# Two attention-and-FFN layers: DMA transposes for the second FFN's levels, its down product behind the next queries, and a new order at both ends of the first FFN

## The chip, the cores and the metric

One NeuronCore of a Trainium2 chip runs the whole kernel. The metric is the device time of one execution in microseconds; below it is the median of three runs.

## The reference

The input is `x` (8 x 256 x 512) with a context of the same shape. Two layers follow each other. Only what the change touches is shown.

```python
# layer 0: causal attention over context and self keys (16 heads of 128, 4 kv heads), then
h = bitlinear(x, w1)                    # w1 2048 x 512, ternary weights, 8-bit activations
x = x + bitlinear(square(relu(h)), w2)  # w2 512 x 2048
# layer 1: single-head attention over the 256 context rows, only the 54 largest scores kept
scores = coef * (x @ Wq.T) @ ctx.T ; thr = top_k(scores, 54)[-1]
x = x + softmax(where(scores < thr, -inf, scores)) @ ctx @ Wo.T
# layer 1: gated FFN with quantized activations
g = silu(bit_linear(x, w_gate)) * bit_linear(x, w_up)          # 2048 wide
x = x + bit_linear(rms_norm(g, ln_weight), w_down)
# in each quantized product: levels = round(x * 127 / max|x|), weights = clip(round(w / mean|w|), -1, 1)
```

## The kernel before

The 2048 rows are 16 tiles n of 128 rows, or 8 pairs (the attention of both layers works on pairs). Each engine runs a program that is written out by hand, in order, and the engines meet only in semaphores; no engine can pass a wait of its own. All DMAs are issued from one queue, SyncE's (SP), which is just as strictly in order. There are three stages.

1. **First attention**, from 0 to about 878 us. It is not changed.
2. **First FFN** (`ffn0`), to about 1189 us. For each tile: `pe_y` multiplies the attention's output by `wo` in four parts (L1349), `dve_norm` adds and normalizes (L1517 is the first step, L1534 the last, which rounds to levels `xh`), `pe_x_turn` transposes them (L1366), `act_xq` copies them out of PSUM (L1463), `pe_up` is the first product (L1378), VectorE takes the maxima (L1562), `act_relu` and `act_square` follow on ScalarE, `dve_hh` rounds, a DMA transposes (`sp_h_turn`, L1288, two of 128 x 1024 a tile), `pe_down` is the second product (L1389) and `dve_x2` adds it to the row. Into this the second layer's three weight matrices are woven: 48 visits k, in each of which SP loads a chunk of 512 KB (`sp_w`, L1269) into one of three slots and ScalarE passes over it (`act_l`, L1438 for the sums of absolute values, L2666 and L2668 for the levels). The slots held chunks 4 to 6 of the first layer's own second weight until ScalarE had made levels of them.
3. **Second layer** (`layer1`), to the end. Its loop runs over s. In a round s the queries and scores of pair s, the rest of the attention of pair o = s - 1, and the gated FFN of the tiles n = 2(s - 2) and n + 1 are interleaved. Per round TensorE does, in this order: gate and up products of tile n (L1925, four quarters j; the first half of the next queries, `pe_xb(s, 0)`, L1828, before j = 2), the way down of tile n - 1 (L1952), the transpose of the masked weights (`pe_xd`, L1859, which waits for `dve_pm`, L2276), the second half of the queries (`pe_xb(s, 1)`), the weighted sum (`pe_xe`, L1875), transposes, scores (L1844), the output product (`pe_xf`, L1890), gate and up of tile n + 1, and the way down of tile n. A quarter j may start only when VectorE's `dve_h` (L2309) of quarter j - 2 has freed its PSUM banks. On VectorE the six rounds that find the 54th largest score (L2265, L2268) are spread over the two gate-and-up passes: rounds 0 to 2 of pair s over that of tile n + 1, rounds 3 to 5 over the next tile's, and `dve_pm` comes after them. Rounds with everything in them are s = 3 to 7.

The FFN's levels `hh` (fp16) are made in two halves, by `pool_levels` (L2507) and `act_levels` (L2110). `pe_h_turn` transposes each half with eight matmuls into PSUM (L1945, between the quarters of the next tile's gate and up), and `act_hT` (L2116) copies it from there to `hT`, which `pe_down` reads.

## Time and profile before

| | |
|---|---|
| median of three runs | 1566.73 us (1563.74 to 1568.1) |
| profiled execution | 1566.82 us, its span 1565.5 us |
| TensorE busy | 1491.3 us, 95% |
| VectorE, ScalarE, GpSimd busy | 73%, 61%, 44% |
| mean granted TensorE clock | 0.986 of 2.4 GHz |

Times on the profile's axis run from the first instruction to the last; the profiled execution took 1.3 us more than that span. Busy time overlaps, since matmuls are pipelined: the rate of an engine is read from the starts of its instructions, not from their lengths.

### The profile page before, as it was taken

The numbers are of one execution on the slowest core, as the hardware profiler recorded it, in microseconds if no ns is written. First come the engines' busy times: TensorE is split into PE (matmuls) and PEld (weight loads), VectorE is DVE, ScalarE is ACT, GpSimd is POOL, SyncE is SP. The second block draws the span as 40 slices with busy tenths as digits, with TensorE's granted clock in tenths as the row PEclk, the third lists the DMA queues.
The fourth block names the chain that finished last, engine by engine and source line by source line (L and its number), as shares of the span: only waits on it lengthen the run. The fifth ranks groups of instructions, "written<-read, shape, count | busy, mean of one in ns | idle before, by whom it ended". The sixth has DMA issues, their size and how long they took to land. (4 is left out here: it accounts for less than half of the span.)

```text
span 1565.5 us, 26196 instructions
## 1 busy us (share of the span) xinstructions
PE 1491.3 (95%) x8637; PEld 1166.0 (74%) x8637; DVE 1136.6 (73%) x2966; ACT 960.5 (61%) x2470; POOL 693.6 (44%) x832
## 2 busy tenths in 40 slices
PE   7999999999999999999999969999998799999988
PEld 6778888888888888888887636666666566666653
DVE  6787787777776877777787735565566988888774
ACT  5666666666666666666667725555555676666655
POOL 4565555555555555556576200000005455555444
PEclk9999999999999999999999988999998999999999
DMA  7011111111111111111336767888785301111000
GB/s 277 27 42 55 41 68 41 41 68 48 48 59 45 60 42 41 68 45 51 122 125 265 266 184 232 273 273 253 254 233 171 110 21 55 55 48 41 28 14 28
DMA packets 84327, 165.09 MB, mean 105 GB/s; under 512 B 39392, under 2 KB 39520, under 8 KB 82784
## 3 DMA queue, kind: packets, MB, share of 16 engines
q1 hardware_dynamic: 84192, 163.41, 30.6%
q8 instruction: 70, 1.15, 0.3%
q14 instruction: 65, 0.53, 0.1%
HBM read 113.05 MB, written 41.94 MB: 99 GB/s over the span
## 5 line engine op out<-in xcount | busy, mean ns | idle before, releaser
L617 ACT ACTIVATE Pt<-Pt,small 128x384 f32<-128x384 f32 (+1 forms) x256 | 173.1, 684 | 106.0 <-DVE small L877 105.9
L368 PE MATMUL bank<-wq,xT 128*128 128x512 f32 x768 | 208.2, 406 | 0.8 <-DVE wq L772 0.8
L421 PE MATMUL bank<-PT,vv 128*128 128x512 f32 x672 | 199.4, 405 | 5.0 <-DVE PT L862 4.1
L1135 POOL TENSOR_SCALAR Pt<-Pt,small 128x384 f32<-128x384 f32 (+1 forms) x256 | 164.8, 657 | 78.9 <-DVE small L885 78.9
L877 DVE CUSTOM_DVE_ANT_0 Pt<-quad,mask,small 128x384 f32<-128x384 f32 (+1 forms) x256 | 171.7, 680 | 30.5 <-PE quad L398 29.1
L1349 PE MATMUL bank<-wq,ot 128*128 128x512 f32 x768 | 181.8, 394 | 1.4 <-DVE xr L1517 1.4
L862 DVE TENSOR_TENSOR PT<-quad,PT 128x512 fp32r<-128x512 f32 x224 | 153.8, 687 | 38.4 <-ACT PT L609 38.0
L1349 PEld LDWEIGHTS bank<-wq,ot 128*128 128x128 f32 x768 | 143.8, 188 | 33.3 <-issue 1.5
L368 PEld LDWEIGHTS bank<-wq,xT 128*128 128x128 f32 x768 | 137.8, 190 | 26.3 <-DVE wq L772 1.9
L1123 POOL TENSOR_TENSOR t<-t 128x512 f32<-128x512 f32 x64 | 83.7, 1308 | 144.2 <-DVE t L843 144.2
L1635 POOL TENSOR_TENSOR cl<-cl,fixed 128x1 f32<-128x1 f32 x16 | 8.8, 552 | 296.4 <-DVE cl L1523 296.4
L421 PEld LDWEIGHTS bank<-PT,vv 128*128 128x128 f32 x672 | 116.4, 189 | 29.3 <-DVE PT L862 10.5
L609 ACT CAST PT<-quad 128x512 fp32r<-128x512 f32 x224 | 128.9, 591 | 7.5 <-PE quad L408 7.5
L408 PE MATMUL quad<-fixed,Pt 128*128 128x128 f32 x896 | 129.4, 273 | 0.6 <-POOL Pt L1135 0.6
L408 PEld LDWEIGHTS quad<-fixed,Pt 128*128 128x128 f32 x896 | 109.6, 140 | 24.3 <-POOL Pt L1135 2.0
L625 ACT CAST OT<-bank 128x512 fp32r<-128x512 f32 x64 | 37.6, 588 | 137.9 <-PE bank L421 137.9
L2521 POOL TENSOR_TENSOR bhw<-bh,lnw 128x512 f32<-128x512 f32 x64 | 81.9, 1279 | 81.8 <-DVE bh L2309 81.7
L396 PE MATMUL quad<-kT,qT 128*128 128x384 f32 (+1 forms) x256 | 99.3, 388 | 2.2 <-DVE small L877 0.8
L1129 POOL TENSOR_TENSOR small<-small,fixed 128x4 f32<-128x4 f32 x64 | 66.2, 1034 | 72.3 <-DVE small L849 72.2
L338 PE MATMUL bank<-wkc,cT 128*128 128x256 f32 x744 | 97.0, 287 | 0.6 <-issue 0.6
L338 PEld LDWEIGHTS bank<-wkc,cT 128*128 128x128 f32 x744 | 90.8, 191 | 8.2 <-DVE vv L828 7.0
L338 PE MATMUL bank<-wkv,xT 128*128 128x256 f32 x744 | 96.5, 286 | 0.0
(286 smaller groups left out, 3504.9 us busy)
## 6 DMA issues: line engine op xcount, KB each, us to landing
ot_scratch<-OT SPq DMA_DIRECT2D x64, 512.0 KB, 2.6
ot<-ot_scratch SPq DMA_DIRECT2D x64, 512.0 KB, 5.3
wkv_f<-in_w SPq DMA_DIRECT2D x12, 512.0 KB, 6.3
wkc_f<-in_w SPq DMA_DIRECT2D x12, 512.0 KB, 6.5
wkv_f<-in_wg SPq DMA_DIRECT2D x11, 512.0 KB, 7.2
wkv_f<-in_wd SPq DMA_DIRECT2D x11, 512.0 KB, 7.1
wkv_f<-in_wu SPq DMA_DIRECT2D x10, 512.0 KB, 7.2
stg<-in_ctxT SPq DMA_DIRECT2D x16, 256.0 KB, 4.4
```

Of the source, the lines that this page charges most:

```text
L338: ins = pe.matmul(kv_bank(u)[:, t * 256:t * 256 + 256], src[i][:, k, t * 128:t * 128 + 128], w[j][:, g, k, :], start=(n == 0), stop=(n == 11))
L368: ins = pe.matmul(bQ[:], xT[p][:, k, qt * 128:qt * 128 + 128], wq[j][:, g, k, :], start=(part == 0 and k == 0), stop=(part == 2 and k == 3))
L396: pe.matmul(bank[:, 0:n], qh, kh, start=True, stop=False)
L408: ins = pe.transpose(bP[k % 2][:, h * 128:h * 128 + 128], Pt[i % 2][:, h, kt * 128:kt * 128 + 128], idf[:])
L421: ins = pe.matmul(bO[:], vv[x][:, bg % 2, kt, :], PT[y][:, k % 2, :], start=(kt == 0 and n == 0), stop=(kt == tiles_in(i) - 1 and n == 2))
L609: act.copy(PT[0][:, k % 2, :], bP[k % 2]).then_inc(f["pt_hi"], 1)
L617: act.activation(p, p, ACT.Exp, bias=nm[:, i % 2, h:h + 1], scale=-1.0, accum_out=sm[:, i % 2, h:h + 1]).then_inc(f["s_exp"], 1)
L862: dve.tensor_tensor(PT[1][:, k % 2, :], bP[k % 2], PT[0][:, k % 2, :].bitcast(F32), ALU.subtract).then_inc(f["pt_lo"], 1)
L877: dve.tensor_tensor_reduce(Pt[i % 2][:, h, 0:n], bS[h % 2][:, 0:n], mask[:, 512 - n:512], scale=cq[:, i % 2, h:h + 1], scalar=3.0e38, op0= ...
L1123: pool.tensor_tensor(t1[:], t1[:], t2[:], ALU.add).then_inc(f["q_add"], 1)
L1135: pool.tensor_scalar(p, p, ri[:, i % 2, h:h + 1], 1.0, ALU.mult, ALU.mult).then_inc(f["p_n"], 1)
L1349: ins = pe.matmul(y_bank(n)[:], ot[:, c % 4, i, k * 128:k * 128 + 128].bitcast(F32R), wo[j][:, g, k, :], start=(g == 0 and k == 0 and q == ...
```

## The change

**First FFN, its beginning.** The tiles' products with `wo` change PSUM banks (odd tiles in bank 3, even ones in bank 0), so that tile 1's needn't wait for tile 0's to be read. The first weight chunks are loaded earlier, each as soon as its own slot is free, and in smaller groups: chunk 0 before tile 2's row, 1 and 2 before the first DMA transposes, 3 before tile 1's transposes, 4 and 5 after tile 3's row, 6 to 8 before tile 2's transposes. ScalarE's passes over them move: chunk 0 from before tile 1's `act_xq` to behind it, chunks 3 to 5 apart (3 ahead of tile 2's `act_xq`, 4 and 5 behind it).

**First FFN, its end.** For tile 14 the order becomes transpose, up, the last parts of tile 15's `wo` product, then the way down of tile 13 and seven filler matmuls; VectorE's `dve_x2(13)` moves to the end of tile 14's work.

**Second layer.** For tiles 0 to 14 two DMA transposes (`sp_h_turn`) of 128 x 1024 fp16 into a new buffer `hL` take the place of the 16 transposes on TensorE, and `act_hT` copies from `hL`. Only tile 15 keeps `pe_h_turn`. In SP's queue they stand before the stores of tile n - 1 and of tile n. `act_hT` of tile n - 1 moves from the quarters 2 and 3 to before the last silu, and to behind the whole pass; that of tile n stays before the silus 1 and 2 of the next pass. The way down of tile n - 1 moves behind `pe_xd` and the second half of the queries, and `dve_x4(n - 1)` behind VectorE's work on these queries.

```diff
@@ -27,6 +27,7 @@
...
 PRODUCTS = ((0, 0), (1, 0), (0, 1))
+HT_BASE = (32, 16)
@@ -1222,7 +1223,7 @@
     def y_bank(n):
-        return banks[3] if n and n % 2 == 0 else banks[0]
+        return banks[3] if n % 2 else banks[0]
@@ -1260,7 +1261,7 @@
...
             if k < 3:
-                sp.wait_ge(f["w_ter"], 16)
+                sp.wait_ge(f["t_lev"], 2 * mem["shared"] - 6 + 2 * k)
             elif seq[k - 3][0] == "A":
@@ -1294,26 +1295,30 @@
...
             sp_ot(c)
+        sp_w([0])
         sp_x(2)
...
         sp_ot(13)
+        sp_w([1, 2])
         sp_h_turn(0, 0)
         sp_h_turn(0, 1)
-        sp_w(range(3))
         sp_ot(14)
         sp_ot(15)
+        sp_w([3])
         sp_h_turn(1, 0)
...
         sp_ot(16)
-        sp_w(range(3, ends[3]))
+        sp_w([4, 5])
         sp_ot(17)
...
             sp_ot(4 * n + 10)
+            if n == 2:
+                sp_w([6, 7, 8])
             sp_h_turn(n, 0)
@@ -1341,8 +1346,8 @@
...
         if g == 0:
-            after(pe, f["x1"], 1 if n == 1 else n - 1)
-            if n == 2:
+            after(pe, f["x1"], n - 1)
+            if n == 1:
                 pe.wait_ge(f["o_lo"], NBLK)
@@ -1413,7 +1418,7 @@
...
         pe_y(3, 1)
-        for n in range(2, NT - 1):
+        for n in range(2, NT - 2):
             pe_x_turn(n)
@@ -1422,6 +1427,12 @@
...
             pe_y(n + 2, 1)
+        pe_x_turn(NT - 2)
+        pe_up(NT - 2)
+        pe_y(NT - 1, 2)
+        pe_y(NT - 1, 3)
+        pe_down(NT - 3)
+        mem["pe_keep"](banks[0][:], 7)
         pe_x_turn(NT - 1)
@@ -1479,7 +1490,10 @@
...
             if n == 1:
-                act_l(1)
+                act_l(0)
+            if n == 2:
+                act_l(4)
+                act_l(5)
             if n == NT - 1:
@@ -1498,9 +1512,10 @@
...
             if n == 1:
-                act_l(2)
-            if n < NT - 2:
-                for k in range(1) if n == 0 else range(max(ends[n], 3), ends[n + 1]):
+                for k in (1, 2, 3):
+                    act_l(k)
+            elif n and n < NT - 2:
+                for k in range(ends[n], ends[n + 1]):
                     act_l(k)
@@ -1623,8 +1638,10 @@
...
                     dve_l(k)
-            if 0 < n < NT - 2:
+            if 0 < n < NT - 3:
                 dve_x2(n)
+            if n == NT - 2:
+                dve_x2(n - 1)
@@ -1703,6 +1720,7 @@
...
     xq = sb("bxq", [128, 512], BF16)
+    hL = sb("bhL", [128, 2048], F16)
     def col(n):
@@ -1741,6 +1759,16 @@
...
+    def sp_h_turn(n):
...
+        if n >= NT - 1:
+            return
+        for j in range(2):
+            sp.wait_ge(f[("hh_v", "hh_a")[j]], n + 1)
+            after(sp, f["h_tT"], 2 * n - 1 + j)
+            sp.dma_start_transpose(hL[:].rearrange("p (k n) -> p k n", k=16)[:, 8 * j:8 * j + 8, :],
+                                   hh[:, 1024 * j:1024 * j + 1024]).then_inc(f[f"b_ht{j}"], 16)
     def sp_head():
@@ -1762,6 +1790,7 @@
...
             if g_:
+                sp_h_turn(n - 1)
                 sp_store(n - 1)
@@ -1771,6 +1800,7 @@
...
             if f_:
+                sp_h_turn(n)
                 sp_store(n)
@@ -1848,11 +1878,8 @@
     def pe_xd(b):
         pe.wait_ge(f["pm"], 2 * b + 2)
-        if b >= 2:
-            pe.wait_ge(f["h_tT"], 2 * (2 * b - 3) + 1)
-        else:
-            pe.wait_ge(f["xat_lo"], min(2 * b + 4, NT))
-            after(pe, f["b_xq"], 1 if b == 1 else 0)
+        pe.wait_ge(f["xat_lo"], min(2 * b + 4, NT))
+        after(pe, f["b_xq"], 2 * b - 1)
         for k in range(2):
@@ -1899,23 +1926,18 @@
...
         else:
-            if n:
-                pe.wait_ge(f["h_tT"], 2 * (n - 2) + 1)
-            else:
-                pe.wait_ge(f["ap_lo"], 1)
+            pe.wait_ge(f["xat_lo"], min(n + 6, NT))
+            pe.wait_ge(f["ap_lo"], n // 2 + 1)
             bank = bT[:].bitcast(F16)
...
-    def pe_gate_up(n, hook, q=None):
+    def pe_gate_up(n, q=None):
         pe.wait_ge(f["b_xq"], n + 1)
...
                 pe_xb(q, 0)
-            for m, part in hook:
-                if part[0] == j:
-                    pe_h_turn(m, part[1])
             u = 2 * (j % 2)
@@ -1926,20 +1948,13 @@
...
-    def pe_h_turn(n, j):
-        pe.wait_ge(f["hh_a" if j else "hh_v"], n + 1)
-        b, odd = divmod(n, 2)
+    def pe_h_turn(j):
...
+        pe.wait_ge(f["hh_a" if j else "hh_v"], NT)
         if j == 0:
-            if odd and b + 1 < NB:
-                pe.wait_ge(f["b_xq"], n + 2)
-            elif odd:
-                pe.wait_ge(f["h_tT"], 2 * n - 1)
-            else:
-                pe.wait_ge(f["xat_lo"], min(2 * b + 8, NT))
-                pe.wait_ge(f["ap_lo"], min(b + 2, NB))
+            pe.wait_ge(f["b_xq"], NT)
         else:
-            pe.wait_ge(f["b_xq"], n + 1 + (1 - odd))
-            after(pe, f["x4"], n)
+            pe.wait_ge(f["x4"], NT - 1)
         bank = (bT, bM)[j][:].bitcast(F16)
@@ -1947,8 +1962,10 @@
...
     def pe_down(n):
-        pe.wait_ge(f["h_tT"], 2 * n + 2)
+        after(pe, f["x4"], n)
         for k in range(16):
+            if k % 8 == 0:
+                pe.wait_ge(f["h_tT"], 2 * NT if n == NT - 1 else 2 * n + k // 8 + 1)
             ins = pe.matmul(bM[:], hT[:, k * 128:k * 128 + 128], wd[k // 4][:, k % 4 * 512:k % 4 * 512 + 512],
@@ -1973,19 +1990,19 @@
...
             if f_:
-                pe_gate_up(n, ((n - 1, (2, 0)), (n - 1, (3, 1))) if g_ else (), s if x_ else None)
+                pe_gate_up(n, s if x_ else None)
             elif g_:
...
                 mem["pe_keep"](bA[0][:], 6)
-                pe_h_turn(n - 1, 0)
-                pe_h_turn(n - 1, 1)
+                pe_h_turn(0)
+                pe_h_turn(1)
                 mem["pe_keep"](bA[0][:], 5)
-            if g_:
-                pe_down(n - 1)
             if o_:
...
                 pe_xb(s, 1)
+            if g_:
+                pe_down(n - 1)
             if o_:
@@ -2006,7 +2023,7 @@
...
             if f_:
-                pe_gate_up(n + 1, ((n, (1, 0)), (n, (2, 1))))
+                pe_gate_up(n + 1)
             if s == 1:
@@ -2106,15 +2123,19 @@
     def act_levels(n):
...
         act.wait_ge(f["hw"], 4 * n + 4)
-        after(act, f["b_ht"], 2 * n)
+        after(act, f["b_ht1"], HT_BASE[1] + 16 * n if n else 0)
         act.activation(hh[:, 1024:2048], hw[:, 1024:2048], ACT.Copy, bias=MAGIC,
...
     def act_hT(n, j):
-        act.wait_ge(f["b_ht"], 2 * n + j + 1)
+        if n == NT - 1:
+            act.wait_ge(f["b_ht"], j + 1)
+            src = (bT, bM)[j][:].bitcast(F16)
+        else:
+            act.wait_ge(f[f"b_ht{j}"], HT_BASE[j] + 16 * (n + 1))
+            src = hL[:, j * 1024:j * 1024 + 1024]
         after(act, f["b_down"], n)
-        act.activation(hT[:, j * 1024:j * 1024 + 1024], (bT, bM)[j][:].bitcast(F16), ACT.Copy,
-                       bias=-MAGIC).then_inc(f["h_tT"], 1)
+        act.activation(hT[:, j * 1024:j * 1024 + 1024], src, ACT.Copy, bias=-MAGIC).then_inc(f["h_tT"], 1)
     def act_gate_up(n, hook, levels=None, q=None, m=None):
@@ -2158,7 +2179,9 @@
...
             if f_:
-                act_gate_up(n, ((n - 1, (2, 0)), (n - 1, (3, 1))) if g_ else (), n - 1 if g_ else None, s if x_ else None)
+                act_gate_up(n, ((n - 1, (3, 0)),) if g_ else (), n - 1 if g_ else None, s if x_ else None)
+                if g_:
+                    act_hT(n - 1, 1)
             elif g_:
@@ -2410,8 +2433,6 @@
...
                 dve_gate_up(n, left, s if x_ else None, None, o if o_ else None)
-            if g_:
-                dve_x4(n - 1)
             if o_:
@@ -2422,6 +2443,8 @@
...
                     dve_qT(s, 1)
+                if g_:
+                    dve_x4(n - 1)
                 if f_:
@@ -2503,7 +2526,7 @@
     def pool_levels(n):
...
         pool.wait_ge(f["hw"], 4 * n + 4)
-        after(pool, f["b_ht"], 2 * n)
+        after(pool, f["b_ht0"], HT_BASE[0] + 16 * n if n else 0)
         pool.tensor_scalar(hh[:, 0:1024], hw[:, 0:1024], col(n)[:, 54:55], MAGIC,
@@ -2617,6 +2640,8 @@
 def block_kernel(nc, a, out):
...
+        f["b_ht0"], f["b_ht1"] = f["x_first"], f["mask_in"]
         ot_dram = nc.dram_tensor("ot_scratch", (NT, 4, 128, 2, 512), F32, kind="Internal").ap()
```

## Rows read from the trace of the kernel before

**Rows 1.** Stretches: length, busy time of each engine, granted clock, DMA share, GB/s
```profile
900.00:920.00 20.00, 12.43 (x48) 6.21 (x47) 5.92 (x16) 7.47 (x12) 0.00 (x0) 0.74 0.64 181
...
996.00:1014.00 18.00, 18.00 (x86) 12.22 (x84) 10.53 (x26) 10.43 (x13) 0.55 (x1) 1.00 0.82 258
...
1249.00:1256.00 7.00, 6.93 (x45) 6.76 (x46) 4.52 (x14) 2.37 (x5) 5.46 (x6) 0.78 0.25 75
...
1309.48:1351.92 42.44, 41.94 (x269) 28.81 (x269) 37.18 (x112) 28.78 (x52) 23.86 (x25) 1.00 0.15 50
```

**Rows 2.** Timeline of TensorE at the first FFN's beginning: start, length, what, idle before
```profile
901.40 0.40 PE L1366 MATMUL bank<-idh,xh 128*128 128x128 f16 x4
901.61 3.01 PE L1349 MATMUL bank<-wq,ot 128*128 128x512 f32 x12
912.17 0.61 PE L1378 MATMUL quad<-wkv_h,xq 128*128 128x512 bf16 x1 [7.55 <-ACT xq L1463]
...
918.26 1.03 PE L1389 MATMUL bank<-wkv_h,wkc_h 128*128 128x512 bf16 x4
...
942.23 0.61 PE L1378 MATMUL quad<-wkv_h,xq 128*128 128x512 bf16 x1 [8.46 <-ACT xq L1463]
...
959.57 0.40 PE L1366 MATMUL bank<-idh,xh 128*128 128x128 f16 x4
```

**Rows 3.** Timeline of ScalarE in the same stretch
```profile
901.38 1.06 ACT L2668 ACTIVATE wkc_h<-wkc_f 128x1024 bf16<-128x1024 f32 x1
910.48 1.06 ACT L1438 ACTIVATE wg<-wkv_f 128x1024 bf16<-128x1024 f32 x1 [8.04 <-DMA wkv_f<-in_wg]
...
938.00 1.06 ACT L1438 ACTIVATE wg<-wkv_f 128x1024 bf16<-128x1024 f32 x1 [14.50 <-DMA wkv_f<-in_wg]
```

**Rows 4.** The first FFN's DMA transposes (L1288), from issue to landing
```profile
DMA to landing us min/median/max: 3.1/3.8/4.3
```

**Rows 5.** Timelines of TensorE and VectorE at the first FFN's end
```profile
1158.71 0.40 PE L1366 MATMUL bank<-idh,xh 128*128 128x128 f16 x4
...
1162.40 0.38 PE L1378 MATMUL quad<-wkv_h,xq 128*128 128x512 bf16 x1
...
1177.55 0.61 PE L1366 MATMUL bank<-idh,xh 128*128 128x128 f16 x4 [6.04 <-DVE xh L1534]
...
1172.84 0.68 DVE L1517 TENSOR_TENSOR xr<-bank,xr 128x512 f32<-128x512 f32 x1
```

**Rows 6.** Timelines of TensorE and GpSimd in one full round of the second layer
```profile
1331.88 1.03 PE L1952 MATMUL bank<-wkv_h,bhT 128*128 128x512 bf16 x4
...
1335.34 0.60 PE L1859 MATMUL bank<-fixed,pm 128*128 128x128 f32 x4
1335.69 3.12 PE L1828 MATMUL bank<-axT,aq 128*128 128x256 f32 x24
...
1353.66 0.61 PE L1945 MATMUL bank<-idh,bhh 128*128 128x128 f16 x8
1354.11 1.03 PE L1925 MATMUL quad<-wg,bxq 128*128 128x512 bf16 x4
...
1346.97 1.12 POOL L2507 TENSOR_SCALAR bhh<-bhw,bcl 128x1024 f16<-128x1024 f32 x1
```

**Rows 7.** Timeline of VectorE in that round: quarter 1 read, weights masked
```profile
1314.98 0.75 DVE L2309 SCALAR_TENSOR_TENSOR bh<-quad,bcl,sg 128x512 f32<-128x512 f32 x1
...
1333.25 0.48 DVE L2276 SCALAR_TENSOR_TENSOR pm<-sc,bcl,pm 128x256 f32<-128x256 f32 x1
```

**Rows 8.** Timeline of TensorE in the first round with gate and up
```profile
1249.07 1.12 PE L1859 MATMUL bank<-fixed,pm 128*128 128x128 f32 x4 [2.73 <-DVE pm L2276]
1249.84 4.08 PE L1828 MATMUL bank<-axT,aq 128*128 128x256 f32 x24
```

**Rows 9.** Timelines of GpSimd and ScalarE before the last tile's pass
```profile
1543.25 1.12 POOL L2507 TENSOR_SCALAR bhh<-bhw,bcl 128x1024 f16<-128x1024 f32 x1 [1.60 <-DVE bcl L2336]
...
1545.08 1.02 ACT L2116 ACTIVATE bhT<-bank 128x1024 bf16<-128x1024 f16 x1 [0.18 <-PE bank L1945]
```

## The prediction

> **What bounds the kernel.** I read the page's busy shares first (they stand in the table above), then a table of stretches, then the timelines of TensorE and of whatever it waited for. TensorE is busy for 95% of the span, so a change of some length must take work off TensorE or close its gaps, and the table says where gaps are. In the middle of the first FFN there are none: 18.00 of 18.00 us are busy at full clock, while in 900 to 920 us only 12.43 of 20 are, at a mean granted clock of 0.74 [rows 1]. A full round of the second layer takes 42.44 us, of which TensorE is busy for 41.94, but VectorE is at 37.18, 88% [rows 1]: a second bound close below. Whether that second bound holds is a matter of order, not of sums, and it decides this change.
>
> **First FFN, beginning.** TensorE waits twice for the transposed levels of a tile: 7.55 us before `pe_up(1)` and 8.46 us before `pe_up(2)`, each time for `act_xq` [rows 2]. ScalarE's timeline has the cause: its last pass over the first layer's weights starts at 901.38, tile 1 is transposed at 901.40, but before `act_xq(1)` stands the pass over chunk 0, which waits 8.04 us for its DMA; chunk 3, ahead of `act_xq(2)`, waits for 14.50 us [rows 2, 3]. The change takes chunk 0 and chunks 4 and 5 out of that place and loads all earlier. Step by step:
>
> - `act_xq(1)` can run at 902.44 (901.38 + 1.06). TensorE's next part of the `wo` product, begun at 901.61, takes 2.9, so `pe_up(1)` starts at about 904.5 instead of 912.17. It also ran at the low level of the clock: its sixteen matmuls took 6.09 us, to the way down's start at 918.26 [rows 2], and sixteen of the same size take 3.46 at the full one (1331.88 to 1335.34) [rows 6]. It ends at about 908.0, 10.3 earlier.
> - `pe_down(0)` needs the DMA transposes, issued at 902.9 behind chunks 1 and 2. Such a transpose lands after 3.1 to 4.3 us [rows 4]; with a megabyte in front of it I estimate 7, so about 1 us of the gain is lost there: 9.1 at tile 2's transpose.
> - The wait before `pe_up(2)` goes, since chunk 3 is issued as soon as the last `wo` part of tile 2 is done, at about 915, and lands before tile 2 is transposed at 921 or just after, under the 3.46 us of `pe_down(1)`. That is 8.46 more, and about as much for the low clock of that `pe_up` as for the one before (2.6 to 2.8), together 20.4.
> - Chunks 4 and 5 now stand before tile 2's relu. SP issues them only after tile 3's row, which waits for the store of tile 0, so at about 923, and they land 6 to 7 us later. Relu, square and rounding of tile 2 then end at about 936, the normalization of tile 3 takes 4.7, and TensorE finds tile 3's levels 1.4 to 1.8 us late.
>
> Tile 3's transpose, at 959.57 [rows 2], comes at about 941: 18.6 us gained. From there to tile 14 the stretches are like the one shown, without a gap to lose it in [rows 1]. The DMA engines have to move in 43 us what took them 62; the middle of the stage shows 258 GB/s at a share of 0.82 [rows 1], so it fits, with little room. Bounds: 20.4 with no wait left, 14 if every chunk lands 2 us later than I take. The bank change buys nothing: tile 0's transpose waits for VectorE anyway.
>
> **First FFN, end.** Tile 14's way down stood between its transpose at 1158.71 and its up product at 1162.40, and everything up to tile 15's transpose hangs on that product's end: maxima, squares, rounding, two normalizations of the next stage, then `dve_norm(15)` at 1172.84, and TensorE waits 6.04 us for it [rows 5]. Now up(14) starts as soon as `act_xq(14)` is done, about 1.1 us after the transpose, so 2.6 earlier; tile 13's way down fills the wait. Without the gap the clock should stay up, and up(15), half of which ran at the low level, is 1.7 to 1.9 shorter if so. I take 3.7, between 2.5 and 4.5.
>
> **Second layer, what is removed.** Eight transposes take 0.45 us of TensorE (1353.66 to 1354.11) [rows 6]; 30 groups of 16 tiles' 32 go, 13.5 us. Would all of it count, the kernel gained 13.5 here. Two things take it away.
>
> - Of the four groups in a round, two lie in the pass of tile n + 1. There TensorE's quarter 3 must wait for `dve_h` of quarter 1, which VectorE finishes at 1315.7 (1314.98 + 0.75) [rows 7], because the output's addition, a scale, a selection round and a normalization come before it without a gap. TensorE began the pass at 1309.48 [rows 1] and starts quarter 3 at 1315.8 now; three quarters of 1.73 us would be ready at 1314.7. The 0.9 us saved turn into a wait.
> - The other two lie in the pass of tile n, which ends at 1331.88 [rows 6], and would end 0.9 earlier, at 1331.0. What follows now is the way down of tile n - 1, 3.46 us, and `pe_xd` at 1335.34 [rows 6]. `dve_pm` is finished at 1333.73 (1333.25 + 0.48) [rows 7]: 1.6 us ahead, hidden by that way down. After the change `pe_xd` comes first. The cover is gone and TensorE waits from 1331.0 to 1333.8, 2.8 us.
>
> VectorE has no idle time between the output's addition, just after 1309.48, and 1333.73, and nothing in this stretch is removed from it. So a round becomes a chain: 24.3 us from the pass's start to `pe_xd` (1333.8 - 1309.48), then what now runs from `pe_xd` to the next pass's start, 16.58 (1351.92 - 1335.34), plus the 3.46 us of the way down that moved in: 44.3 us for 42.44 [rows 1, 6, 7]. TensorE's own work in a round falls to about 40, so VectorE's chain decides. That is 1.9 us slower in each of five rounds, 9.5. In round 8, which has no next queries, `pe_xd` already came right behind `dve_pm`, and the moved product covers part of two evictions: 1.2 slower. Together 10.7; nothing if `dve_pm` turned out to come early enough, 13 at most, as the slack of 1.6 differs a little by round.
>
> **Second layer, the DMA transposes.** Tile n's levels are ready at 1348.1 (1346.97 + 1.12), and TensorE transposes their first half at 1353.66, so nobody asks for them earlier now [rows 6]. By the median of 3.8 [rows 4] the first DMA transpose lands at 1351.9, the second some 1.3 later (an estimate of its issue), and it is due a silu, a square and an `act_xh` later than the first. Tile n - 1's land when ScalarE comes to them, and the moved product needs them 4 us later. Both are covered. SP's queue: the transposes of n stand behind the store of n - 1, which now comes 5 us later, and the loads behind that store; they have 3 us to spare. ScalarE's copy now reads SBUF instead of PSUM; its passes of that width from SBUF take 1.06 [rows 3], the copy takes 1.02 [rows 9], which costs nothing on an engine two thirds busy [rows 1].
>
> At the end the cover is missing. Tile 14's levels are finished at 1544.37 (1543.25 + 1.12), and the copy to `hT` starts at 1545.08 [rows 9]. By DMA it starts 3.8 after the levels, about 1548.2, 3.1 late, and ScalarE's silu 1, with the last tile's whole pass, stands behind it. Before, tile 13's second half, now behind its pass, delays `dve_x4(13)`, on which tile 15's transpose hangs, by 1.5. I take 4.6, between 2 and 7.
>
> **Sum.** 1566.8 (the profiled execution; the median of the runs is 1566.7) - 18.6 - 3.7 + 10.7 + 4.6 = 1559.8, say 1560 us. About 0.3% is what a measurement of this kernel can tell from no change, 4.7 us either way.
>
> **Rivals.**
>
> - *The clock falls at each wait for the weights.* In the first round with gate and up, a wait of 2.73 us before `pe_xd` was followed by 4 transposes in 1.12 for 0.60 and 24 matmuls in 4.08 for 3.12 [rows 6, 8], the stretch at a granted clock of 0.78 [rows 1]. From start to start that is 1.4 us. Six new waits of 2.8 or more: 8.4, so 1568. For it: the equal length. Against it: TensorE had also idled in the microseconds before that one, and the new waits follow full work; waits of 1.4 to 1.8 elsewhere left the clock up. [...]
> - *The beginning gives back what it gains.* If chunk 3 can't come sooner than now, its pass stays at 938.0 [rows 3], `act_xq(2)` stays behind it, and tile 3 gains only the 2.4 us of the two passes that moved: 1576, slower by 0.6%. The place is ScalarE ahead of `act_xq(2)`; from a gain of less than 6.9 at the beginning the kernel is slower than before by over 0.3%. For it: SP stands in line, each load behind stores and rows. Against it: chunk 3 is put in front of the stores, and the mean rate around these waits is 181 GB/s for 258 in the middle [rows 1].
> - *The removed transposes count.* If VectorE's chain gave way by over 1.9 us a round, rounds would be shorter than 42.4, at best by the four groups' 1.8, 9 in five rounds and 2 in the others: 1566.8 - 18.6 - 3.7 - 11 + 4.6 = 1538. Against it: VectorE is without a gap in that stretch.
> - *Only the beginning moves*, the clock at the end of the first FFN falls nevertheless and the tail costs 7: 1566.8 - 18.6 - 2.5 + 10.7 + 7 = 1563.
>
> **Chances.** The forecast with its bounds 0.47, the clock 0.25, the beginning 0.13, the transposes 0.07, the last 0.08. The range, 1551 to 1572, leaves out the transposes' case and the ends of two others. The forecast's own range is 1553 to 1566. Faster by over 0.3% (below 1562.0): 0.49, most of the forecast's case and the transposes'; within 0.3%: 0.33, the rest of it, the last case and most of the clock's; slower: 0.18, the beginning's case and the clock's with a smaller gain at the beginning.
>
> **What would show it.** Right: tile 3's transpose near 941, no wait over 2 us before `pe_up(1)` and `pe_up(2)`; rounds of about 44.3 us with a wait of 2.8 before the transpose of the masked weights and one of about 1 before quarter 3; VectorE at 84% in a round; the copy to `hT` of tile 14 waiting for a DMA for over 2 us. Wrong: rounds under 42 us; a low clock behind each wait for `dve_pm`, with rounds of 45.7; ScalarE waiting for a weight DMA ahead of `act_xq`. The largest error would come from the beginning, which rests on landing times under a load that the trace does not show.

## The result, and the profile after

The changed kernel takes 1573.76 us (median of five runs, 1571.95 to 1577.62), the kernel before 1564.81 (five runs, 1563.4 to 1568.1). The ratio is 1.006, with a 95% interval of 1.0044 to 1.0076: slower by 0.6%, 9 us, where 1560 was forecast. The profiled execution took 1576.41 us (span 1575.1), 9.6 more than that of before. TensorE is busy for 1479.2 us, 12 less than before, so work did leave it; the time went into waits.

The two profiles are compared at five landmarks. (Line numbers of the changed kernel differ: its `pe_x_turn` is L1371 and `pe_up` L1383 in the first FFN, `pe_down` L1394; in the second layer `pe_xd` is L1886, the gate and up products L1947, the way down L1969, the copy to `hT` L2138.)

| landmark | before | after | after minus before |
|---|---|---|---|
| tile 4's transpose, behind the beginning | 977.75 | 964.34 | -13.4 |
| second layer's first queries | 1189.20 | 1181.91 | -7.3 |
| pass of tile 1, where the first full round starts | 1267.04 | 1259.69 | -7.3 |
| the same pass in round 7, where the last full round ends | 1478.77 | 1484.55 | +5.8 |
| end | 1565.5 | 1575.1 | +9.6 |

So the beginning gained 13.4, the first FFN's end lost 6.1, the five full rounds lost 13.1 and the rest 3.8.

**Beginning.** TensorE's timeline, to be held against [rows 2]:

```profile
883.21 0.61 PE L1371 MATMUL bank<-idh,xh 128*128 128x128 f16 x4 [2.49 <-DVE xh L1549]
...
905.07 0.39 PE L1383 MATMUL quad<-wkv_h,xq 128*128 128x512 bf16 x1
...
911.12 1.02 PE L1394 MATMUL bank<-wkv_h,wkc_h 128*128 128x512 bf16 x4 [2.43 <-DMA wkc_h<-hh]
...
924.10 1.02 PE L1394 MATMUL bank<-wkv_h,wkc_h 128*128 128x512 bf16 x4 [0.93 <-DMA wkc_h<-hh]
...
927.55 0.38 PE L1383 MATMUL quad<-wkv_h,xq 128*128 128x512 bf16 x1
...
944.77 0.61 PE L1371 MATMUL bank<-idh,xh 128*128 128x128 f16 x4 [2.68 <-DVE xh L1549]
...
945.17 1.91 PE L1394 MATMUL bank<-wkv_h,wkc_h 128*128 128x512 bf16 x4
...
964.34 0.40 PE L1371 MATMUL bank<-idh,xh 128*128 128x128 f16 x4
```

Both long waits for `act_xq` are gone (905.07 and 927.55 have none). In their place stand four short ones: 2.49 before tile 0's transpose, two for DMA transposes, 2.68 for tile 3's levels, the last with a low clock behind it (four matmuls of the way down in 1.91 for 1.03). ScalarE's timeline has the cause of the last:

```profile
934.24 1.06 ACT L1449 ACTIVATE wg<-wkv_f 128x1024 bf16<-128x1024 f32 x1 [1.05 <-DMA wkv_f<-in_wg]
...
935.29 2.04 ACT L1479 ACTIVATE r<-quad 128x512 f32<-128x512 f32 x4
```

Tile 2's relu stands behind chunk 5, which lands at 934.2. The DMA transposes' own times from issue to landing, for tile 0's and for those after 948 us:

```profile
DMA to landing us min/median/max: 5.7/6.0/6.2
...
DMA to landing us min/median/max: 3.4/3.8/4.6
```

And two stretches of the beginning, with the columns of [rows 1]:

```profile
898.00:912.00 14.00, 11.57 (x56) 7.41 (x55) 8.01 (x24) 9.63 (x13) 0.56 (x1) 1.00 0.97 289
...
930.00:948.00 18.00, 15.32 (x66) 10.83 (x65) 7.92 (x22) 10.37 (x17) 0.55 (x1) 0.91 0.97 288
```

Where chunks and transposes meet, the DMA engines are full: a share of 0.97 at 289 and 288 GB/s, and tile 0's DMA transposes take 5.7 to 6.2 us and tile 2's 4.8 to 5.3 in place of 3.8.

**First FFN's end.** TensorE's timeline, to be held against [rows 5]:

```profile
1161.54 0.40 PE L1371 MATMUL bank<-idh,xh 128*128 128x128 f16 x4 [1.08 <-DVE xh L1549]
...
1173.24 0.61 PE L1383 MATMUL quad<-wkv_h,xq 128*128 128x512 bf16 x1 [10.86 <-ACT xq L1474]
...
1181.91 3.22 PE L1858 MATMUL bank<-axT,aq 128*128 128x256 f32 x24
```

Tile 15's transpose comes 1.08 after TensorE is free (6.04 before), as meant. Then its up product waits 10.86 for `act_xq(15)`. ScalarE:

```profile
1170.70 1.99 ACT L2041 CAST aq<-aq_in 128x1024 fp32r<-128x1024 f32 x2 [16.65 <-DMA aq_in<-in_aq]
...
1172.59 0.59 ACT L1474 ACTIVATE xq<-bank 128x512 bf16<-128x512 f16 x1
```

Its copy stands behind the cast of the query weights (`aq`), and that waited 16.65 for a load. SP's queue:

```profile
1162.48 0.32 SPq L1274 DMA_DIRECT2D x_scratch<-xr  x1
...
1162.91 2.68 SPq L1289 DMA_TRANSPOSE wkc_h<-hh  x2
...
1165.65 0.57 SPq L1779 DMA_DIRECT2D aq_in<-in_aq  x1
```

The load was issued at 1165.65, behind tile 14's DMA transposes, and these behind the store of tile 13, which waits for `dve_x2(13)`. VectorE:

```profile
1161.71 0.75 DVE L1603 SCALAR_TENSOR_TENSOR xr<-bank,cl,xr 128x512 f32<-128x512 f32 x1
```

That is the addition which the change moved behind tile 15's normalization. The load's own condition, the end of tile 15's last `wo` part, was met at 1155.5.

**Second layer.** Two rounds, with the columns of [rows 1]:

```profile
1259.69:1304.11 44.42, 40.18 (x237) 26.99 (x237) 37.09 (x112) 29.05 (x52) 23.85 (x25) 1.00 0.30 74
...
1304.11:1350.04 45.93, 41.67 (x238) 28.44 (x237) 37.19 (x112) 29.06 (x52) 23.83 (x25) 0.96 0.28 69
```

TensorE in the second of them:

```profile
1310.41 1.04 PE L1947 MATMUL quad<-wg,bxq 128*128 128x512 bf16 x4 [0.95 <-DVE bh L2332]
...
1328.42 0.66 PE L1886 MATMUL bank<-fixed,pm 128*128 128x128 f32 x4 [2.64 <-DVE pm L2299]
...
1328.83 4.61 PE L1858 MATMUL bank<-axT,aq 128*128 128x256 f32 x24
```

The five full rounds take 44.42, 45.93, 45.91, 44.43 and 44.17, before 42.44 each (the last 41.96). The waits stand where the prediction put them: 0.95 before quarter 3, 2.64 for `dve_pm`. VectorE's share is 37.09 of 44.42. The two long rounds differ from the others by what follows the wait: 24 matmuls in 4.61 us here and 4.25 in the other, 3.12 in the other three [rows 6]. TensorE is busy for 1.5 us longer with the same work, at a granted clock of 0.96 for 1.00.

**Tail.** TensorE around the last pass:

```profile
1557.17 1.04 PE L1947 MATMUL quad<-wg,bxq 128*128 128x512 bf16 x4 [2.48 <-DVE bh L2332]
```

and ScalarE's copy of tile 14, in front of the silu on which VectorE waits:

```profile
1554.64 1.06 ACT L2138 ACTIVATE bhT<-bhL 128x1024 bf16<-128x1024 f16 x1 [2.75 <-DMA bhL<-bhh]
```

The copy waits 2.75 for its DMA transpose, and quarter 3 starts 2.48 late. From round 8's second pass to the end it is 51.3 us, before 48.4.

### The profile page after: what moved, and what is told of

The parts are those of the page before. It is cut to its first block and busy times, and to the rows that moved or that the text cites. A ratio compares the mean times of both kernels' runs of the same rounds, so it can differ in the third digit from the quotient of the medians.

```text
span 1575.1 us, 25773 instructions
## 1 busy us (share of the span) xinstructions
PE 1479.2 (94%) x8404; PEld 1154.6 (73%) x8404; DVE 1136.5 (72%) x2966; ACT 962.0 (61%) x2470; POOL 693.9 (44%) x832
## 5 line engine op out<-in xcount | busy, mean ns | idle before, releaser
L878 DVE CUSTOM_DVE_ANT_0 Pt<-quad,mask,small 128x384 f32<-128x384 f32 (+1 forms) x256 | 171.5, 679 | 30.5 <-PE quad L399 29.1
```

The costliest lines, as they stand in the source:

```text
L878: dve.tensor_tensor_reduce(Pt[i % 2][:, h, 0:n], bS[h % 2][:, 0:n], mask[:, 512 - n:512], scale=cq[:, i % 2, h:h + 1], scalar=3.0e38, op0= ...
```

## The experiments

Each median is of 4 to 12 executions, timed beside the kernel before, whose median was 1565.23, 1564.66 and 1564.5 in the three groups. Gains "by medians" are differences of these medians and of the changed kernel's 1573.76.

| kernel | median us | ratio to before, 95% |
|---|---|---|
| beginning_alone | 1549.13 | 0.9903 (0.989 to 0.9916) |
| ffn_ends_alone | 1557.61 | 0.9959 (0.9947 to 0.9971) |
| layer1_alone | 1581.0 | 1.0097 (1.0084 to 1.0111) |
| xq_before_aq | 1574.49 | 1.0056 (1.0043 to 1.0068) |
| aq_load_first | 1566.02 | 1.001 (1.0 to 1.0019) |
| relu_before_chunks | 1575.38 | 1.0069 (1.0057 to 1.0081) |
| down_before_weights | 1557.14 | 0.9959 (0.9943 to 0.9974) |
| fill_before_weights | 1573.24 | 1.005 (1.0038 to 1.0062) |
| one_round_less | 1572.52 | 1.0053 (1.0036 to 1.0069) |
| tile14_on_tensore | 1572.3 | 1.0046 (1.0032 to 1.0059) |
| loads_first_down_first | 1545.54 | 0.9878 (0.9865 to 0.9891) |
| loads_first_old_layer | 1545.59 | 0.988 (0.9867 to 0.9892) |

### The parts by themselves

**beginning_alone** and **ffn_ends_alone** put the changed first FFN, without and with its end, ahead of the old second layer; **layer1_alone** is the other half.

> Only the beginning of the first FFN is changed; its end and the second layer are those of before. Theory: the gain up to tile 4 is 13.4 us and all of it is kept, since the wait of 10.86 us before the last up product came from moving the last-but-two tile's way down and its addition: span 1552, faster by 0.85%. Rival (the second layer's first weight matrix can't come sooner whatever stands ahead of it in the queue): the wait for it grows here too and the gain is 7 to 8 us, as with both ends.

> The changed first FFN, both ends, with the second layer of the kernel before. Theory (the three parts add up, and the second layer lost by itself): the profiles of before and after give 13.4 us gained up to tile 4 (977.75 against 964.34), 6.1 lost at the end of the first FFN, so 7.3 gained where the second layer's queries begin, and nothing lost from there: 1565.5 - 7.3 = 1558 us of span, faster by 0.5%. Rival (the second layer's loss came from starting it out of step with its loads, not from its own edits): some of the 17 us is lost here too, and the span is 1562 or more.

> Only the second layer is changed; the first FFN is that of before. Theory (the loss of the second layer is its own): 13.1 us in five full rounds, of which 3 hang on the clock and may come as 10 to 16, 1 in round 8 and 2.9 at the end: 14 to 20 slower, span 1582. Rival (the loss came from the two halves of the change together, the transfers of the first FFN's late end running into the second layer's): 10 or less.

By medians: 16.1 faster for the beginning, 7.6 for both ends, 16.3 slower for the second layer. The parts add up (-7.6 + 16.3 = +8.7, measured +9), and the rivals of ffn_ends_alone and layer1_alone, which had the second layer's loss come from outside it, fall. The end costs 8.5. The beginning alone did better than expected, span 1547.3 for 1552: its tile 4 was transposed at 961.30, 3 us earlier than in the profile after. Over the executions profiled with these edits that landmark lies between 961.3 and 965.8; the clock after tile 0's and tile 3's waits falls in some and not in others. The beginning is worth 12 to 16.5, and the profile after showed one of its poorer cases.

### The wait at the first FFN's end

**xq_before_aq** moves ScalarE's copy ahead of the cast:

```diff
@@ act_program, n == NT - 2, then n == NT - 1 behind act_xq(n)
-                l1["act_w"](0)
-                l1["act_w"](1)
...
+                l1["act_w"](0)
+                l1["act_w"](1)
                 l1["act_xT"](0)
```

> The changed kernel with one edit: ScalarE copies the last tile's levels before it casts the query weights, not behind the cast. Theory: the 10.86 us wait before the last up product is ScalarE's queue, where the cast waits for its load behind tile 13's store on SP; with the copy ahead the product starts 10 us sooner, and the next bound is the cast itself, then the transposed rows: the queries begin at about 1176 for 1181.9, 6 us gained, span 1569. Rival (TensorE's own order, the way down behind the product, holds the queries anyway or the clock falls in the gap): under 2 us gained.

Nothing was gained. TensorE:

```profile
1164.08 0.39 PE L1383 MATMUL quad<-wkv_h,xq 128*128 128x512 bf16 x1 [0.25 <-ACT xq L1474]
...
1176.69 1.09 PE L1835 MATMUL bank<-fixed,axn 128*128 128x128 f32 x4 [10.71 <-DVE axT L2250]
```

The up product starts at once, and inside it the transpose of the next stage's rows waits 10.71, since ScalarE's `act_xT(0)` now stands behind the same cast. My theory took the queue for the cause; the wait only went to the next customer. The load has to come sooner, which **aq_load_first** does:

```diff
@@ sp_program (first FFN)
             if n == NT - 2:
                 l1["sp_head"]()
+                l1["sp_weights"]()
             sp_store(n - 1)
...
-        l1["sp_weights"]()
```

> The changed kernel with the loads of the second layer's weights moved ahead of tile 13's store on SP; ScalarE's order is as changed. Theory (the load stands behind the store that the change made 6 us later): the last wo part ends at 1155.5, so the load is issued there for 1165.65 and lands 5 us later at about 1161, the cast ends at 1163, the wait of 10.86 us before the last up product shrinks to 1 or 2, and the queries begin at about 1170.5 for 1181.9: 11 us gained, span 1564. Rival A (the DMA transposes of tile 14, now behind the weights, come late and hold the way down that follows): half of it, 5 to 6. Rival B (the casts have another cause of being late): under 2.

7.7 us gained by medians. TensorE's timeline:

```profile
1161.09 0.39 PE L1383 MATMUL quad<-wkv_h,xq 128*128 128x512 bf16 x1 [0.53 <-ACT xq L1474]
...
1167.29 1.47 PE L1394 MATMUL bank<-wkv_h,wkc_h 128*128 128x512 bf16 x4 [2.14 <-DMA wkc_h<-hh]
...
1172.24 3.22 PE L1858 MATMUL bank<-axT,aq 128*128 128x256 f32 x24
```

and SP's:

```profile
1153.71 0.33 SPq L1779 DMA_DIRECT2D aq_in<-in_aq  x1
...
1160.67 0.33 SPq L1274 DMA_DIRECT2D x_scratch<-xr  x1
1161.11 14.19 SPq L1289 DMA_TRANSPOSE wkc_h<-hh  x4
```

The wait of 10.86 is 0.53. But tile 14's DMA transposes still stand behind tile 13's store, which waits for the moved addition until 1160.67. They are issued at 1161.11, behind a second load of 1 MB from 1158.54, take 5.4 to 6.0 us to land, and the way down finds them 2.14 late. Rival A named the load in front of them; that they stand behind the store is a second cause, which it didn't name. The last two kernels put the transposes right behind the load:

```diff
@@ sp_program (first FFN); sp_aq is the wait and the first load of sp_weights
                 l1["sp_head"]()
+                l1["sp_aq"]()
+                sp_h_turn(n, 0)
+                sp_h_turn(n, 1)
             sp_store(n - 1)
```

> The changed first FFN with the query weights' load and tile 14's DMA transposes ahead of tile 13's store, and the second layer of the kernel before. Theory: 12 us below the 1557.6 that the changed first FFN gave with the second layer of before, 1545.6; and against it the other kernel of this group shows what the DMA transposes of the second layer are worth by themselves: 5 rounds by 0.65 less 1.4 at the end, 0 to 3. Rival as there: 1550 or more.

> The changed kernel with two repairs. On SP the query weights' load goes ahead of tile 13's store, and tile 14's DMA transposes right behind that load, so that neither waits for the addition that the change moved back. In the second layer the way down of tile n - 1 stands ahead of the masked weights again. Theory (the losses are these two orders, not the DMA transposes or the beginning): the load alone gave 7.9 of span with 2.14 of wait and about 1.8 of low clock left at the way down of tile 14, so about 12; the old place of the way down gives 16.6 by medians against the changed kernel: 1573.8 - 12 - 16.6 = 1545. Rival (the first FFN's end can't use an earlier load, since the next stage waits for the rows): 1549 or more.

TensorE in the second of them:

```profile
1161.77 0.39 PE L1387 MATMUL quad<-wkv_h,xq 128*128 128x512 bf16 x1 [0.50 <-ACT xq L1478]
...
1165.67 1.03 PE L1398 MATMUL bank<-wkv_h,wkc_h 128*128 128x512 bf16 x4
...
1168.93 3.22 PE L1866 MATMUL bank<-axT,aq 128*128 128x256 f32 x24
```

Both measured 1545.5 to 1545.6, as expected. From tile 14's transpose to the first queries it is 30.5 us before (1158.71 to 1189.20), 36.6 after, 28.8 with the load first and 24.75 here. In this stretch the new order of the end is worth 5.7, once SP's queue follows it. By medians it is less: loads_first_old_layer is 18.9 below its kernel before and beginning_alone 16.1, so 2.8. And no run moves the loads alone in the old order, where up(15) also waits, 1.37 us, for a copy behind the same cast; so how much of the gain is the earlier load's isn't shown.

### The wait that moved in the beginning

**relu_before_chunks** takes chunks 4 and 5 from ahead of tile 2's relu:

```diff
@@ act_program
-            if n == 2:
-                act_l(4)
-                act_l(5)
             for j in range(4):
                 act_relu(n, j)
+            if n == 2:
+                act_l(4)
             for j in range(2):
                 act_square(n, j)
+            if n == 2:
+                act_l(5)
```

> The changed kernel with ScalarE's passes over chunks 4 and 5 moved, from ahead of tile 2's relu to ahead of and behind its squares. Theory (tile 3's levels are 2.5 to 2.7 us late since relu stands behind a pass whose load lands at 934): the wait before tile 3's transpose goes, and the low clock after it: tile 4's transpose comes 2.5 to 4.1 earlier, the span 1571 to 1572.5. Rival (the copy of tile 3's levels now stands behind passes that moved back, as tile 1's did before the change): no gain, or a loss of 1 to 3.

TensorE's timeline:

```profile
940.15 0.40 PE L1371 MATMUL bank<-idh,xh 128*128 128x128 f16 x4
...
944.04 1.48 PE L1394 MATMUL bank<-wkv_h,wkc_h 128*128 128x512 bf16 x3 [3.50 <-DMA wkc_h<-hh]
...
962.89 0.40 PE L1371 MATMUL bank<-idh,xh 128*128 128x128 f16 x4
```

and the landing of tile 2's DMA transposes:

```profile
DMA to landing us min/median/max: 5.8/7.0/8.2
```

The wait before tile 3's transpose is gone, and 3.50 stand before the way down of tile 2 instead: its DMA transposes, issued right behind three chunks, took 5.8 to 8.2 us. Tile 4 comes at 962.89, within the others' scatter. Neither theory had this. Here a better order on ScalarE only shows the next transfer, a transpose behind 1.5 MB of chunks.

### The second layer's rounds

**down_before_weights** puts the cover back:

```diff
@@ pe_program
+            if g_:
+                pe_down(n - 1)
             if o_:
                 pe_xd(o)
             if x_ and s != 1:
                 pe_xb(s, 1)
-            if g_:
-                pe_down(n - 1)
@@ act_program (and in dve_program dve_x4(n - 1) goes back ahead of dve_pT(o))
-                act_gate_up(n, ((n - 1, (3, 0)),) if g_ else (), n - 1 if g_ else None, s if x_ else None)
-                if g_:
-                    act_hT(n - 1, 1)
+                act_gate_up(n, ((n - 1, (3, 0)), (n - 1, (3, 1))) if g_ else (), n - 1 if g_ else None, s if x_ else None)
```

> The changed kernel with the way down of tile n - 1 put back ahead of the masked weights' transpose, and VectorE's addition back with it; the DMA transposes stay. Theory (the way down was the cover for VectorE's chain): no wait for pm is left, the quarter 3 wait of 0.95 stays, each full round takes 41.6 us (two of four groups of removed transposes count), 2.9 less than the 44.4 and 4.4 less than the two rounds with the clock low: the span is 14 + 4 = 18 us shorter, about 1557. Rival A (the DMA transposes are the loss: they land late and the way down waits for them): rounds stay at 43 or more. Rival B (VectorE's chain sets the round whatever the order): 42.4 to 44.

One round, with the columns of [rows 1]:

```profile
1382.57:1424.11 41.54, 39.97 (x234) 26.94 (x237) 37.01 (x112) 29.02 (x52) 23.73 (x25) 1.00 0.25 65
```

and its quarter 3 and masked weights on TensorE:

```profile
1388.65 1.04 PE L1947 MATMUL quad<-wg,bxq 128*128 128x512 bf16 x4 [0.95 <-DVE bh L2330]
...
1407.31 0.60 PE L1886 MATMUL bank<-fixed,pm 128*128 128x128 f32 x4
```

The round takes 41.54, 41.6 expected: no wait for `dve_pm`, the 0.95 before quarter 3 still there. (The first two rounds take 42.13 and 42.17, as ScalarE's second copy to `hT` is 0.4 to 0.5 late.) 16.6 us gained by medians, so the moved way down (with the addition and the copy that moved with it), not the DMA transposes, made the second layer slower. And by loads_first_old_layer, with the same median and rounds of 42.44, the DMA transposes are worth nothing in sum, and in the two profiles they are 1.4 us behind: 3.3 won in five rounds (208.4 for 211.7) goes again at the tail (50.6 for 48.4) and between the first queries and the first full round (79.3 for 76.5, in part the clock).

**fill_before_weights** keeps TensorE busy in the wait:

```diff
@@ pe_program
+            if o_ and f_:
+                after(pe, f["x4"], n - 1)
+                mem["pe_keep"](bM[:], 11)
             if o_:
                 pe_xd(o)
```

> The changed kernel with eleven filler matmuls (2.4 us) ahead of the transpose of the masked weights in each round, where TensorE waits 2.64 for VectorE. Theory (the 1.5 us that two of five full rounds took over the others is the clock that fell in this wait): every round takes 44.4 or a little under, none 45.9, the first round's 2.74 wait too: the span is 3 to 4 us below the changed kernel's profile, 1571.5, and the runs scatter less. Rival (the long rounds are chance of another kind, or the fillers delay the weights): no less than 1574.

TensorE in one round:

```profile
1323.14 2.54 PE L2728 MATMUL bank<-ones 128*128 128x512 bf16 x11
...
1325.94 0.66 PE L1886 MATMUL bank<-fixed,pm 128*128 128x128 f32 x4 [0.26 <-DVE pm L2302]
...
1326.35 3.12 PE L1858 MATMUL bank<-axT,aq 128*128 128x256 f32 x24
```

The full rounds take 44.42, 44.42, 44.43, 44.42 and 44.19, and the runs lie between 1571.31 and 1573.57 where the changed kernel's spread over 5.7 us. The span of 1570.6 is 4.5 below the profile after, 3 of it in the rounds, but by medians the gain is only 0.5. That the fillers did it isn't shown: without any, four other executions with this second layer have no long round either. TensorE in layer1_alone:

```profile
1336.39 0.66 PE L1870 MATMUL bank<-fixed,pm 128*128 128x128 f32 x4 [2.64 <-DVE pm L2283]
1336.81 3.12 PE L1842 MATMUL bank<-axT,aq 128*128 128x256 f32 x24
```

So it is in all five full rounds of layer1_alone, xq_before_aq, aq_load_first and relu_before_chunks. Only the profile after (two rounds) and tile14_on_tensore (three) have long ones: 5 of 30 such waits, for none of 5 with fillers. Fillers or not, a low clock is rare enough here that one execution can't tell. The 1.5 us of a long round are the clock's, as the rows of the two rounds after the change show; whether fillers remove them stays open.

**one_round_less** shortens VectorE's chain, by leaving out one of the six selection rounds:

```diff
@@ dve_program
-   left = [(o, r) for r in range(4 if s == 2 else 3, 6)] if o_ and s > 1 else []
+   left = [(o, r) for r in range(4, 6)] if o_ and s > 1 else []
```

> The changed kernel, leaving out part of the computation: from the third pair on, VectorE's fourth selection round of six isn't made, 1.57 us of VectorE ahead of the masked weights (1323.06 to 1324.63 in the profile after). TensorE's work is the same. Theory (VectorE's chain from the pass's start to the masked weights sets the round): each full round takes 44.42 - 1.57 = 42.85 us, the wait before the transpose of the weights is 1.07 for 2.64, and the clock stays up: with six such rounds 9 to 10 us less, 12 to 13 against a profile in which the clock fell twice: span 1563 to 1566. Rival (TensorE waits there for something else, or the wait reappears elsewhere in the round): rounds of 44 or more, span over 1570.

The rounds were 43.85 (three of five; 45.38 and 44.85 with the clock low), only 0.57 shorter, and the wait is 2.06 for the 1.07 expected. VectorE's `dve_pm` in one round:

```profile
1369.33 0.47 DVE L2299 SCALAR_TENSOR_TENSOR pm<-sc,bcl,pm 128x256 f32<-128x256 f32 x1
...
1369.73 1.47 DVE L2299 SCALAR_TENSOR_TENSOR pm<-sc,bcl,pm 128x256 f32<-128x256 f32 x1
```

GpSimd beside it:

```profile
1369.49 1.43 POOL L2544 TENSOR_TENSOR bhw<-bh,lnw 128x512 f32<-128x512 f32 x1 [1.56 <-DVE bh L2332]
```

and TensorE behind it:

```profile
1371.27 0.66 PE L1886 MATMUL bank<-fixed,pm 128*128 128x128 f32 x4 [2.06 <-DVE pm L2299]
```

`dve_pm`'s second instruction took 1.47 for 0.48. With the selection round gone it runs while GpSimd multiplies tile n's quarter, which in the changed kernel was over by then. The chain was shortened by 1.57 - 0.99 = 0.58, and the round by 0.57: the theory holds to 0.01 us and the size I expected was wrong.

### The tail

**tile14_on_tensore** gives tile 14's transposes back to TensorE:

```diff
@@ pe_gate_up (sp_h_turn ends at NT - 2; act_hT reads the banks from n = NT - 2)
+            if n == NT - 1 and j in (1, 2):
+                pe_h_turn(j - 1, NT - 2)
```

> The changed kernel with tile 14's levels transposed by TensorE as before (and tile 15's, as changed), between the quarters of the last tile's pass. Theory (the last DMA transposes had lost their cover): the wait of 2.48 before quarter 3 of the last pass goes, and with it most of the 2.6 us by which the stretch from the last pass to the end had grown: 2 to 2.6 less at the end, 1571.5 to 1574 as the median is 1573.8. Rival (the wait before quarter 3 is VectorE's own): under 0.7.

TensorE in the last pass:

```profile
1555.63 0.62 PE L1963 MATMUL bank<-idh,bhh 128*128 128x128 f16 x8 [0.53 <-POOL bhh L2539]
```

No wait is left before quarter 3, and from round 8's second pass to the end it is 48.8 us for 51.3, 2.5 less. The median is only 1.5 lower; this profile, the slowest of the five, had three long rounds of 45.7 to 45.9.

## Why the prediction was wrong, step by step

- **First FFN, beginning:** 18.6 forecast, 13.4 in the profile after and 12 to 16.5 over all profiled executions with these edits. `pe_up(1)` came at 905.07 (904.5 forecast) and `pe_up(2)` without a wait, both right. Chunk 3, issued at 917.90 for 915, landed at 923.05, and ScalarE waited 8.26 for it ahead of `act_xq(2)`, one of my signs of being wrong; the way down hid it. Mis-sized: tile 0's DMA transposes landed within the 7 I allowed, but were issued at 904.8 for 902.9, and for tile 1's I allowed nothing, so two waits (2.43, 0.93) where I had one of 1; tile 3's levels came 1.6 to 3.4 late for 1.4 to 1.8. "The bank change buys nothing" was wrong to the other side: it made one wait of 2.49 (883.21) out of two of 1.44 and 0.93, and after it the clock fell in seven of the twelve profiled executions with this change, the profile after among them: up(0) started at 887.64 for 886.63. "It fits, with little room" held as a mean (253 GB/s over 898:948) and failed where it counted, at a share of 0.97. relu_before_chunks shows how little the order on ScalarE changes there.
- **First FFN, end: the step that failed.** I wrote that tile 13's way down "fills the wait" and took 3.7 as a gain; it was a loss of 6.1. I followed the moved product on TensorE, where the forecast came true (tile 15's transpose came 16.24 us after tile 14's for 18.84, the 2.6 forecast), but not what waits for its addition: `dve_x2(13)`, the store, and behind it in SP's queue two DMA transposes and the second layer's first load. That put a wait of 10.86 before up(15). I had named such queues for the second layer and skipped them here. aq_load_first and loads_first_old_layer show the cause, and that a gain is there (5.7 in the stretch, 2.8 by medians, for 3.7) once the queue is put in order too, in part perhaps the load's own.
- **Second layer:** right in mechanism and nearly in size. Rounds of 44.42 (44.3 forecast), waits of 2.64 (2.8) and 0.95 (1), round 8 at +0.95 (1.2). The sum is 14.1 for 10.7, because the clock fell in two of five rounds, 3.0. This was the first rival, for a part: with a chance per round, not always. The same wait stands in every round, but three of five are at a granted clock of 1.00. The Trainium skill ("TensorE: Matmul & The Clock Gate", section "HAM oscillation — how this bites in real kernels") tells of a kernel that was throttled after every one of its waits, of about 3 to 5 us each. That doesn't carry over to the waits of 2.6 to 2.9 us here, of which 5 in 30 lowered the clock.
- **Tail:** 2.9 for 4.6, inside 2 to 7; the copy waited 2.75 (3.1 forecast), and `dve_x4(13)` cost 0.3, not 1.5.

Sum: 1559.8 forecast, 1576.4 profiled. Of the 16.6 between them the end of the first FFN makes 9.8, the beginning 5.2, the second layer's rounds 3.4 (3.0 of it the clock), the tail -1.7. The second rival (1576) had the number and not the place. The range, to 1572, held no case in which the end itself lost.

What stays open is why the clock falls after one wait of 2.64 us and not after the next; the same waits, 0.95 and 2.64, stand in both kinds of round. The 3.0 us that it took from the profile after are that execution's: four of the six without fillers lost none in their full rounds.

## What to carry to other kernels

When a product moves later, follow its result past the engines: who stores it, and what stands behind that store in the DMA queue. Here the load that the next stage's first casts waited for stood behind one store, and came 20.3 us after tile 14's transpose for 13.7 before, and moving one customer ahead of the cast only moved the wait. And work between a slow chain on another engine and the wait for it is cover: taking it away cost 16.6 us here, more than all the transposes that were removed.

## What the runs showed of the hardware

- VectorE's 128x256 masked multiply took 1.47 us instead of 0.48 when it ran beside GpSimd's 128x512 multiply (1.43 us, from 1369.49 to 1370.92), and ended 0.3 after that; its neighbour, which had begun before GpSimd's, took 0.47. The Trainium skill has this ("SBUF — State Buffer", "Who interferes with whom"): an instruction of VectorE's with two SBUF inputs and one of GpSimd's that reads SBUF exclude each other, and the later one is blocked until the other ends. The rows agree: the instruction that began second was the one held up, about until GpSimd's end. Whether other pairs of instructions do this wasn't tried.
- The same idle time of 2.64 us was followed by 24 matmuls in 3.12 us in three rounds of the profile after and in 4.61 and 4.25 us in two. Over the six profiled executions with waits of 2.63 to 2.89 us in the full rounds and no fillers, 5 of 30 rounds were long, in two of the executions; with eleven fillers in the wait, none of five.
- DMA transposes of 128x1024 took 3.8 us from issue to landing at a DMA share of 0.82 [rows 1, 4], 4.8 to 6.2 at 0.97, and up to 8.2 right behind 1.5 MB of loads.
